# An fp32 mixing kernel built by masking instead of by bf16 parts and copies, with the start-up re-ordered around it

## What is computed

```
h   = gelu(gelu(cond @ W0 + b0) @ W1 + b1);  att = softmax(h @ W2 + b2)      (64 samples, K = 8)
agg = einsum('bk,koi->boi', att, weight);    agg_b = att @ bias_k            (a 64x64 matrix per sample)
m   = einsum('boi,bih->boh', agg, x) + agg_b[:, :, None]
q   = fp8(m / s_m), s_m = max|m| / 448;      w = fp8(W.T / s_w), s_w = max|W| / 448
x   = x + (q @ w) * s_m * s_w + bias
```

## Time and profile before

| | |
|---|---|
| median of 3 runs | 527.64 us (527.1 to 528.81) |
| the profiled execution | 530.63 us, of which 528.8 are the span of the profile |
| TensorE busy | 510.2 us, 96% |
| VectorE busy | 414.1 us, 78% |
| ScalarE busy | 244.2 us, 46% |
| GpSimd busy | 59.3 us, 11% |

### The profile page before, as it was taken

One profiled execution on the slowest core, in us unless ns is written; L12 is line 12 of the kernel. 1 busy time (PEld: TensorE's weight loads), 2 busy tenths in 40 slices (PEclk: granted clock), 3 DMA queues, 4 the chain that ended last, 5 costly groups with the idle time before them and its releaser, 6 DMA issues.

```text
span 528.8 us, 9489 instructions
## 1 busy us (share of the span) xinstructions
PE 510.2 (96%) x3480; PEld 284.7 (54%) x3512; DVE 414.1 (78%) x524; ACT 244.2 (46%) x286; POOL 59.3 (11%) x68
## 2 busy tenths in 40 slices
PE   5799999899999999999999999999999999999997
PEld 4444454355555555555555555555555555555563
DVE  7799999877877777777777777777777777777652
ACT  3469898655344444444444444444444444442310
POOL 5266776011000000000000000000000000000000
PEclk9999999999999999999999999999999999999999
DMA  7999591146666666665656565656656666566532
GB/s 220 382 390 403 206 337 55 58 103 134 189 199 187 183 185 184 182 180 180 180 180 180 180 180 180 180 180 180 180 180 180 183 182 180 181 189 190 193 121 79
DMA packets 85651, 100.61 MB, mean 190 GB/s; under 512 B 34468, under 2 KB 67046, under 8 KB 85638
## 3 DMA queue, kind: packets, MB, share of 16 engines
q1 hardware_dynamic: 84610, 99.41, 59.9%
q0 software_dynamic: 656, 0.82, 0.9%
q10 hardware_dynamic: 372, 0.20, 0.1%
HBM read 58.41 MB, written 32.75 MB: 172 GB/s over the span
## 4 chain that ended last, share of the span: by engine, by line
PE 77%; DVE 12%; DMA 4%; issue 3%; SPq 2%; ACT 1%; POOL 1%; ACTq 0%; DVEq 0%; POOLq 0%
PE pair L1181 40%; PE pair L1155 19%; PE pair L1171 15%; DVE stat L804 5%; DMA Y<-in_L_ffn_weight_dram 2%; DMA work<-work 2%; PE pair L1055 1%; DVE work L729 1%; DVE work L819 1%; DVE work L921 1%; DVE Y L819 1%; DVE work L732 1%; PE pair L1145 1%; SPq L336 1%; POOL fixed L489 1%
## 5 line engine op out<-in xcount | busy, mean ns | idle before, releaser
L1181 PE MATMUL pair<-f1T,work 128*128 128x512 f16 x1024 | 231.0, 379 | 0.0
L1181 PEld LDWEIGHTS pair<-f1T,work 128*128 128x128 f16 x1024 | 98.9, 98 | 113.5 <-DVE work L928 0.2
L608 ACT ACTIVATE work<-Y,consts 128x1024 bf16 (+1 forms) x29 | 33.3, 1148 | 185.7 <-DVE work L902 185.7
L921 DVE TENSOR_TENSOR work<-Y,work 128x512 f16<-128x512 f16 (+1 forms) x64 | 71.2, 1119 | 48.0 <-ACT work L641 46.9
L1155 PE MATMUL pair<-f0T,work 128*128 128x512 bf16 x435 | 98.6, 379 | 1.8 <-DMA work<-work 0.3
L1171 PEld LDWEIGHTS pair<-taps,work 128*128 128x128 f16 x1536 | 88.3, 98 | 8.7 <-issue 0.9
L1171 PE MATMUL pair<-taps,work 128*128 128x128 f16 x1536 | 91.2, 219 | 0.6 <-issue 0.5
L934 DVE TENSOR_TENSOR Y<-pair,Y 128x512 f32 (+1 forms) x64 | 43.9, 686 | 44.4 <-PE pair L1181 44.4
L641 ACT CAST work<-Y 128x512 f16 (+1 forms) x64 | 69.6, 1137 | 19.3 <-DVE Y L911 15.6
L1155 PEld LDWEIGHTS pair<-f0T,work 128*128 128x128 bf16 x464 | 45.3, 98 | 55.1 <-DMA work<-work 0.6
L1055 PE MATMUL pair<-Y,work 128*128 128x512 f32 x128 | 61.2, 613 | 0.4 <-ACT Y L581 0.4
(11 more groups left out here) (157 smaller groups left out, 242.4 us busy)
## 6 DMA issues: line engine op xcount, KB each, us to landing
Y<-in_x_dram SPq DMA_DIRECT2D x64, 512.0 KB, 3.9
out_dram<-Y SPq DMA_DIRECT2D x31, 512.0 KB, 3.8
split_rows<-work SPq DMA_DIRECT2D x30, 520.0 KB, 2.6
work<-split_rows SPq DMA_DIRECT2D x30, 520.0 KB, 3.9
Y<-in_L_ffn_weight_dram SPq DMA_DIRECT2D x8, 512.0 KB, 9.0
Y<-in_L_ffn_W_q_dram SPq DMA_DIRECT2D x5, 512.0 KB, 15.1
work<-in_L_ffn_W_q_dram SPq DMA_DIRECT2D x3, 512.0 KB, 15.2
work<-work SPq DMA_DIRECT2D x8, 65.0 KB, 3.9
```

What stands on the lines that cost most here:

```text
L921: nc.vector.tensor_tensor(split[:, r, s, 1], v[:, r, :], split[:, r, s, 0], ALU.subtract)\
L1181: last = mm(ps[2 + h][:, :], y1s[n][:, e, k, :], f1T[:, k, h * H:(h + 1) * H], start=False, stop=(e == 1 and k == KT - 1), skip_group_chec ...
```

## The change

The splitting into bf16 parts, the nine copies within SBUF and the parts of att are gone. Instead att is written K x KC = 64 wide, each of its eight columns eight times (attR), turned once, and multiplied by a mask of zeros and ones (own_c) into attM, 64 rows by 8 blocks of 64 columns, so that block c holds att only in the rows of channel group c. Four fp32 products of 512 columns of wkf, as it was loaded, with attM then give all of agg; the layout of the result in PSUM, and so the steps of the eight placing copies, are other ones. The bias product uses attM's first block, with the bias rows spread over 64 rows of a cleared mbk2.

Around it: x tile 0 is loaded before the fifth piece of w0 and x tile 1 before the seventh; the taps' loads are GpSimd's first issues; the sums of the taps are taken before the softmax; nmax goes ahead of the first maximum of w0; three of the eight tap turns go ahead of the products. The turn of w_part moves from behind tile 0 to behind tile 2, the product with w_all from within tile 1 to within tile 3, the turns of zst from behind tile 1 to behind tile 3; two maxima of one tile each (tiles 0 and 1) stand between the steps of that exchange; scale_w0 for round r comes behind tile 3r+2 instead of 3r-1; w0's turns come one tile later; and two of three keep_clock calls are gone. The diff, cut to its core (lines in brackets or with spaces before a remark stand for several):

```diff
@@ layout
         def mix_src(m, par, b):
-            return pair[m][par * C:(par + 1) * C, :].rearrange("p (j t b) -> p b t j", t=T, b=NB)[:, b]
+            return pair[m][par * C:(par + 1) * C, :].rearrange("p (q c t b) -> p b t q c", q=2, c=KC, t=T)[:, b]
         def mix_dst(m, par, b):
-            o = b * C + 32 * m + par
-            return mixw[b * C:(b + 1) * C, :, o:o + 31:2]
+            rows = mixw[b * C:(b + 1) * C, :, b * C:(b + 1) * C]
+            return rows.rearrange("p t (c m q o) -> p m o t q c", c=KC, m=2, q=2)[:, m, par]
...
+        KR = K * KC
+        wkf = work[0:KR, 5 * L:5 * L + KF]
+        attM = work[0:KR, 6 * L:6 * L + KC * B].rearrange("p (c b) -> p c b", c=KC)
...
+        attR = mlp[0:B, 848:848 + KR]
+        own_c = mlp[0:KR, 912:912 + KC]
-        mbk2 = f0T[0:K, R8 - 1, 0:2 * P].bitcast(fp32)
+        mbk2 = f0T[0:KR, R8 - 1, 0:2 * P].bitcast(fp32)
-        groups = [(0, 1)] + [g for r in range(R8) for g in ((3 * r + 1, 2), (3 * r + 3, 1))]
+        groups = [(0, 1), (1, 1), (2, 2)] + [g for r in range(1, R8) for g in ((3 * r + 1, 2), (3 * r + 3, 1))]
-        turns0 = {3 * r + 6: r for r in range(R8)}
+        turns0 = {3 * r + 7: r for r in range(R8)}
@@ SyncE
             for r in range(3):
                 load_w0(r)
-            for e in range(2):
-                sp.wait_ge(wk_parts, (1, 3)[e])
-                for i in range(3):
-                    sp.dma_start(wkp9[3 * i + e:KP:9, :], wkp[:, e, :]).then_inc(ld["wkp"], 16)
             load_w0(3)
+            load_mixing(0)
+            sp.wait_ge(mbk_zero, 1)
+            for b in range(NB):
+                sp.dma_start(mbk2[0:KR:KC, b * C:(b + 1) * C], cbk).then_inc(ld["mbk"], 16)
             load_w0(4)
-            for b in range(NB):
-                sp.dma_start(mbk2[:, b * C:(b + 1) * C], cbk).then_inc(ld["mbk"], 16)
             load_w0(5)
-            load_mixing(0)
+            load_mixing(1)
             load_w0(6)
             load_w0(7)
...
-                if n == 3:
+                if n == 5:
                     sp.wait_ge(mix_mm, 2)
+                    sp.wait_ge(mlp_mm, 6)
                 load_w1(n)
@@ GpSimd
+            for b in range(NB):
+                pool.dma_start(convraw[b * C:(b + 1) * C], convw).then_inc(ld["convw"], 16)
             nc.gpsimd.memset(ident[:, :], 0.0).then_inc(ident_zero, 1)
...
-            for b in range(NB):
-                pool.dma_start(convraw[b * C:(b + 1) * C], convw).then_inc(ld["convw"], 16)
+            nc.gpsimd.memset(mbk2, 0.0).then_inc(mbk_zero, 1)
...
-            pool.wait_ge(wk_parts, 4)
-            for i in range(3):
-                pool.dma_start(wkp9[3 * i + 2:KP:9, :], wkp[:, 2, :]).then_inc(ld["wkl"], 16)
@@ ScalarE
-            act.dma_start(wkf, ...)      first of five issues
+            act.dma_start(wkf, ...)      last of five issues
...
-            act.wait_ge(attp_mm, 1)
-            nc.scalar.copy(attpT, ps[1][:, :].bitcast(bf16)[0:KP, 0:B]).then_inc(attp_ev, 1)
-            act.wait_ge(mlp_mm, 5)
-            nc.scalar.copy(attT, ps[6][0:K, 256:320]).then_inc(mlp_ev, 1)
             act.wait_ge(mixw_zero, 4)
-            for m, par in ((0, 0), (0, 1), (1, 0)):
+            for m in range(2):
                 act.wait_ge(mix_mm, m + 1)
-                for b in range(NB):
-                    ev = nc.scalar.copy(mix_dst(m, par, b), mix_src(m, par, b))
+                for par in range(2 - m):
+                    for b in range(NB):
+                        ev = nc.scalar.copy(mix_dst(m, par, b), mix_src(m, par, b))
                 ev.then_inc(placed_act, 1)
...
-                if t == 1:
+                if t == 3:
                     act.wait_ge(zs_mm, 1)
                     nc.scalar.copy(zs, ps[6][:, 384:384 + P // 2].bitcast(fp16)).then_inc(zs_ev, 1)
-                if t == 2:
+                if t == 5:
                     act.wait_ge(w_step, 2)
-                if t % 3 == 2 and t <= 20:
-                    scale_w0(t // 3 + 1)
+                if t % 3 == 2 and 5 <= t <= 23:
+                    scale_w0(t // 3)
@@ VectorE
-            for n in range(3):
-                clear_mixw(n)
-            dve.wait_ge(ld["wk"], 16)
-            (wkp[0] = bf16(wkf); wkr = wkf - wkp[0]; wkp[1] = bf16(wkr); wkp[2] = wkr - wkp[1])
+            clear_mixw(0)
+            clear_mixw(1)
+            dve.wait_ge(ident_made, 1)
+            nc.vector.tensor_reduce(own_c, ident[0:KR, 0:KR].rearrange("p (k c) -> p c k", k=K), AX.X, ALU.add)\
+                .then_inc(own_made, 1)
+            clear_mixw(2)
+            clear_mixw(3)
+            dve.wait_ge(ld["convw"], 32)
+            dve.wait_ge(tapcols_made, 3)
+            for part in (tapsum, tapsum2):
+                nc.vector.tensor_reduce(part, convraw.rearrange("p c k -> p k c"), AX.X, ALU.add)\
+                    .then_inc(tapsum_red, 1)
...
-            largest_w0(0)
             dve.wait_ge(mlp_mm, 4)
             nc.vector.tensor_reduce(nmax, ps[3][0:B, 0:K], AX.X, ALU.max, negate=True).then_inc(mlp_ev, 1)
+            largest_w0(0)
...
-            nc.vector.tensor_scalar(att, ex, rinv, None, ALU.mult).then_inc(mlp_ev, 1)
-            (four steps that make attp, three bf16 parts of att)
-            clear_mixw(3)
+            nc.vector.tensor_scalar(attR.rearrange("p (k c) -> p k c", k=K),
+                                    ex.unsqueeze(2).to_broadcast([B, K, KC]), rinv, None, ALU.mult).then_inc(mlp_ev, 1)
+            dve.wait_ge(mlp_mm, 5)
+            dve.wait_ge(own_made, 1)
+            nc.vector.tensor_tensor(attM, ps[6][0:KR, 256:256 + B].unsqueeze(1).to_broadcast([KR, KC, B]),
+                                    own_c.unsqueeze(2).to_broadcast([KR, KC, B]), ALU.mult).then_inc(mlp_ev, 1)
...
-            for r in range(1, 5):
+            for r in range(1, 4):
                 largest_w0(r)
             place_last()
-            for r in range(5, R8):
+            for r in range(4, R8):
                 largest_w0(r)
             dve.wait_ge(w_red, R8)
             nc.vector.tensor_reduce(w_part, w_rows, AX.X, ALU.max).then_inc(w_red, 1)
-            (tapsum, tapsum2)
+            largest_mixed(0)
             dve.wait_ge(w_pe, 1)
             nc.vector.tensor_reduce(w_all, ps[7][0:1, 0:P], AX.X, ALU.max).then_inc(w_red, 1)
+            largest_mixed(1)
             dve.wait_ge(w_pe, 2)
...
-                if r == 0:
-                    largest_mixed(0)
-                largest_mixed(2 * r + 1)
+                if r:
+                    largest_mixed(2 * r + 1)
                 largest_mixed(2 * r + 2)
@@ TensorE
             keep_clock(16)
-            (transpose of attp9; transpose of att; keep_clock(12); waits for ld["wkp"], ld["wkl"], attp_ev)
             pe.wait_ge(mlp_ev, 7)
+            nc.tensor.transpose(ps[6][0:KR, 256:256 + B], attR, ident[0:B, 0:B]).then_inc(mlp_mm, 1)
+            turned_tap_rows(range(0, 3))
+            pe.wait_ge(ld["wk"], 16)
+            pe.wait_ge(mlp_ev, 8)
             for q in range(4):
-                for j in range(8):
-                    o2 = 8 * q + j
-                    last = mm(ps[q][:, j * B:(j + 1) * B], wkp9[:, o2 * 2 * C:(o2 + 1) * 2 * C],
-                              attpT, start=True, stop=True)
+                last = mm(ps[q][:, :], wkf[:, q * 2 * C:(q + 1) * 2 * C], attM.rearrange("p c b -> p (c b)"),
+                          start=True, stop=True)
                 if q % 2:
                     last.then_inc(mix_mm, 1)
+            turned_tap_rows(range(3, R8))
             pe.wait_ge(ld["mbk"], 32)
-            mm(ps[6][:, 320:384], mbk2, attT, start=True, stop=True).then_inc(mlp_mm, 1)
+            mm(ps[6][:, 320:384], mbk2, attM[:, 0, :], start=True, stop=True).then_inc(mlp_mm, 1)
...
-            keep_clock(10)
-            pe.wait_ge(placed_act, 3)
+            pe.wait_ge(placed_act, 2)
...
-                if t == 0:     transpose of w_part
+                if t == 2:     transpose of w_part
-                if t == 1:     turns of zst (and, within the tile, the product with w_all)
+                if t == 3:     turns of zst (and, within the tile, the product with w_all)
```

More of the change, by code:

```diff
@@ L106, in adaln_ffn_kernel @@
         mixw = work[:, 0:T * P].rearrange("p (t m) -> p t m", t=T)
-        KP = 9 * K
-        wkp9 = Y[0:KP, 20 * L:22 * L].bitcast(bf16)
         KC = C // K
         KF = C * C // KC
[L113 to L118, removed]
+        KR = K * KC
+        wkf = work[0:KR, 5 * L:5 * L + KF]
+        attM = work[0:KR, 6 * L:6 * L + KC * B].rearrange("p (c b) -> p c b", c=KC)
         wide_taps = f0T[:, 0, 0:CG * R8 * 4].bitcast(fp32).rearrange("p (c j) -> p c j", c=CG)
@@ L130, in adaln_ffn_kernel @@
         mw2 = mlp[:, 832:840]
-        att = mlp[0:B, 840:848]
-        attT = mlp[0:K, 848:912]
+        attR = mlp[0:B, 848:848 + KR]
+        own_c = mlp[0:KR, 912:912 + KC]
         rowb = mlp[0:1, 976:984]
@@ L202, in taps_part @@
```

(56 more changed lines are left out.)

7 lines of the change are left out of this document (removed).

## The result

The changed kernel takes 532.17 us (median of 4 runs, 531.41 to 532.45), the kernel before, run beside it, 528.06: a ratio of 1.0079, 95% interval 1.006 to 1.0098. It is slower by 4.1 us, where 3.4 less were forecast. The profiled execution took 531.41 us, its span is 529.4.

A forecast was written before the change was run, and what follows sets the result against it. Bound: a load until 24.12 us, then VectorE's eight rounds, TensorE a close second. Round two 2.8 us earlier plus 0.6 at the end saves 3.4: 527.64-3.4=524.2 us, range 523.0 to 529.0; forecast's chance 0.47.

The forecast's parts named there:

- Transfers: Start-up loads: without the nine copies within SBUF everything behind lands 5.4 us earlier (4.05+1.4), last w0 piece 4.1.
- The base: Saving of 3.4 us set against the median 527.64, as the profiled execution (530.63) was 3.0 above it.
- 33.2 for round two: Second VectorE round of w0 starts at 33.2 us, 2.8 earlier, after x tile 3's load at 24.1.
- The chain up to the products: Softmax, att's turn and attM before the four new products: attM done at 10.85, products from 10.9.
- Placing: Eight copies of products from PSUM to SBUF: 0.63 us each on ScalarE, tile 0 at 18.2 to 19.0.
- Level of TensorE: TensorE clock from the new products on: passes fall from 0.85 to 0.44 us within them, tiles 1.74 each.
- (b): Rival, start-up: TensorE low through tile 0, round two at 35.3, saving 1.3, 526.4 us; chance 0.14.
- (c): Rival, first tiles: TensorE low over several tiles, 1.7 us each; with three, 2.1 slower, 529.8 us; chance 0.10.
- (a): Rival, placing copies: slow writes, 1.15 us each, tile 0 at 21.4; 527.0 to 528.5 us, middle 527.7; chance 0.23.
- Tile 3's start plus 9.1: First rounds: from tile 3's start through tiles 4 and 5, eviction and scaling to round two, 24.1+9.1=33.2.
- The end: Behind the last w0 round: VectorE's last maxima run without the 0.56 us break for tile 30's eviction; saves 0.6.
- New wait for the scaling: Before round two: VectorE waits 1.1 us for ScalarE's first scale_w0, now behind tile 5's eviction; paid once.

The follow-up runs named there:

- second profile of before: The kernel before, no edit, profiled once more: 528.56 us, span 526.7, 2.1 below the first profile.
- Both mends: Changed kernel with placing copies walked 8 bytes innermost and the four products on 128 rows (added rows zero): median 527.13 us, ratio 0.9976 to the kernel before.
- the run with fast copies: Changed kernel with only the placing copies walked with the two channels 8 bytes apart innermost: ratio 1.0026 to the kernel before.

## Why the prediction was wrong, point by point

- **Transfers: the landings right, the gain not.** Neighbouring landings 5.4 us apart became 1.3, the last w0 piece landed at 19.9 (forecast 20.0), x tile 3 at 23.8 (24.1). But the gain was added up from 4.05, the gap, and 1.4, by which piece 2 was held to be late for the copies. Piece 2 lands at 10.3 in the second profile of before, with the copies, and at 10.4 in the changed kernel, without: the 1.4 were that first execution's and not the copies'. x tile 3 lands at 27.4 there, so the gain was 3.6, not 5.4.
- **The base: wrong.** The prediction saw that the profiled execution stood 3.0 us above the median and set the whole saving against the median all the same. Two of these 3.0 lay in the very loads that it credited to the change. A second profile shows it; the first alone could not. With that base, the prediction's own 33.2 for round two is 34.13-33.2=0.9 us earlier and with 0.6 at the end 1.5 in all. Both mends, with tile 3 bound by its load as forecast, gave 0.0024 of 528.61, or 1.3. So even with copies and level as forecast, less than half of the 3.4 was there to be had.
- **The chain up to the products: right** (10.47 against 10.9). Their price: the bounds were 3.5 to 6.8 us, the chosen second half at 16.0 to 17.7; it was 17.7, all eight passes low.
- **Placing: wrong, and the step that failed first.** 0.63 was taken for a copy and 1.07 measured, so tile 0 came at 20.89, where 18.2 to 19.0 were forecast and the run with fast copies has 19.44. The upper bound (1.135, the strided read L641) was the nearer row, and PSUM's cheap wide reads were no evidence on a write to SBUF. The rule of the Trainium skill (Advanced Engine Details and Errata, SBUF Cachelines) gave the right answer; here a write pays as a read does.
- **Level of TensorE: wrong too.** The forecast had tiles at 1.74 each, 5.2 for three; they took 7.84, 2.6 more, with six of twelve passes low. It was given 0.24 in two rivals, (b) and (c), each with fast copies, and a clause in (a). Rival (a) priced slow copies at tile 3 from 26.8, or 28.2 to 28.5 with the level fallen, rival (c) several low tiles; what came is near the end of (a): tile 0 at 20.9, one and a half low tiles, tile 3 at 28.7. But (a) had the level fall in an idle time of 2 to 4 us, while in fact it had not risen before tile 0, and TensorE stood idle for only 1.38. Copies and level were not independent: the same four products that end late also leave the level low. Tile 3's start plus 9.1, the prediction's own sum, gives 37.8 for round two; 37.97 was measured. Rival (a) makes 528.5 of nearly this trace, 3.7 less than was measured; 1.9 of that is the base (36.06 against 34.13).
- **The end: right by itself, but the rounds took some of it back.** VectorE's last maxima ran without a break. From the eighth round to their end it is 95.34-80.44=14.9 us, against 93.76-77.98=15.8: 0.9 less, where 0.6 were forecast. But rounds two to eight take 42.5 us instead of 41.9, for the most part as round two's first step takes 0.88 instead of 0.42. The net gain was 0.3. New was a longer idle time of TensorE in the exchange (1.51 against 0.96).
- **New wait for the scaling: right in size** (1.07 against 1.1), but it hid GpSimd's hold on VectorE, which the prediction did not have.

Open: that zeros in 64 more rows bring the level up was seen in five profiles, against four in which the 64-row products left it low; the two clears on VectorE came with it and were not tried alone, and why 64 rows leave the level low is not known. From the activation scale to the end the changed kernel is 0.8 us shorter (432.4 against 433.3), but that stretch spreads by as much between profiles of kernels with the same main part (433.1 with both mends).

## What to carry to other kernels

When a copy's layout changes, look at the step of its innermost walk in SBUF, on the write side too, and put the pair that lies 8 bytes apart innermost, as here; that costs two lines. When short or narrow products are replaced, or unused ones removed, ask at which level TensorE is before, and who keeps it up until the next dense work: a mend to one of the two was worth 0.3 to 0.5% here, both together 1.0%. And before a saving is carried from one profile to a median, ask whether the profile's excess lies in the same rows: take a second profile.

## What the runs showed of the hardware

- A copy of 64x512 fp32 from PSUM to SBUF takes 618 ns on ScalarE and 695 on VectorE where the innermost step of the write is 8 bytes, even if only two elements long, and 1026 to 1084 on either with 32 or 512 bytes.
- Eight fp32 passes of 512 columns on 64 rows left TensorE low for 7.16 us of unbroken work; on 128 rows the level rose within them (4.5 to 5.3 us for the eight). It fell in an idle time of 4.05 us and held in one of 1.3.
- The record's granted clock read 1.00 for the low level at the start of the changed kernel (passes 0.85 us apart from 10.47), and 0.66 for the low level after a fall (20 to 25 us, products on 128 rows).
- VectorE's 128x1024 int16 step took 2.04 us instead of 0.43 while GpSimd multiplied a piece of w1, and ended 0.28 us behind it. The Trainium skill (SBUF — State Buffer, Who interferes with whom) says that a VectorE instruction in a two-port mode and GpSimd shut each other out for a whole instruction. The trace agrees, with 31.36+2.04=33.40 against 31.21+1.91=33.12; in which mode the step ran, no view shows.
